# A graph-attention kernel's first stage: order of SyncE's loads and stores, finer query stores, and a block of transposes placed elsewhere on TensorE

## The reference, cut to what matters

```python
h = layernorm(x) @ w_in + b_in             # 3125 x 256
xn = layernorm(h, ln1_g[0], ln1_b[0])
q, k, v = xn @ wq[0] + bq[0], xn @ wk[0] + bk[0], xn @ wv[0] + bv[0]
# then, for each edge: scores from q[dst] and k[src], a softmax over the
# edges of one dst, and the sum of attn * v[src] at dst
```

## Time and profile before

| what | value |
|---|---|
| time, median of 3 runs | 3984.43 us (3982.08 to 3995.94) |
| the profiled execution, time | 4018.18 us |
| its span | 4016.4 us |
| mean granted TensorE clock | 0.733 |
| PE busy in the span | 2360.2 us |
| DVE busy | 2475.5 us |
| ACT busy | 1336.1 us |
| POOL busy | 1837.9 us |
| first gather of the edges | 329.57 us after the span's start |

### The profile page before, as it was taken

The page is one execution under the profiler, slowest core; times in us unless marked ns, Lnnn a source line. Parts: engine busy times, 40 slices in busy tenths (PEclk is TensorE's granted clock), DMA queues, the critical chain, the costliest instruction groups (busy, mean ns, idle before and its releaser), DMA issues. The chain is left out here.

```text
span 4016.4 us, 37654 instructions
## 1 busy us (share of the span) xinstructions
PE 2360.2 (59%) x7337; PEld 1568.5 (39%) x7338; DVE 2475.5 (62%) x3964; ACT 1336.1 (33%) x3899; POOL 1837.9 (46%) x1938
## 2 busy tenths in 40 slices
PE   5863455555555555478773555555555555487697
PEld 3331333333333333256541333333333333366576
DVE  3653777677767777643434777777777777543223
ACT  1111344343434444312112434443434434221132
POOL 4005566666666666221116666666666665111000
PEclk8776676666766667689986666676767667698799
DMA  3226667677666666512126666776666666311100
GB/s 92 64 67 184 180 207 210 197 209 207 207 200 199 203 201 207 149 50 87 60 85 197 199 205 203 208 210 207 206 207 202 203 205 190 90 54 58 43 26 32
DMA packets 293357, 623.34 MB, mean 155 GB/s; under 512 B 51905, under 2 KB 163705, under 8 KB 293184
## 3 DMA queue, kind: packets, MB, share of 16 engines
q0 software_dynamic: 149904, 471.38, 40.4%
q1 hardware_dynamic: 143280, 150.27, 11.8%
HBM read 526.62 MB, written 94.78 MB: 155 GB/s over the span
## 5 line engine op out<-in xcount | busy, mean ns | idle before, releaser
L723 POOL DMA_INDIRECT ring<-kv_table,stage_ix x1760 | 1673.9, 951 | 1020.9 <-issue 601.7
L949 PE MATMUL bank<-qs,hot_q 128*128 x1760 | 710.9, 552 | 616.0 <-issue 304.5
L962 PE MATMUL bank<-ring,hot_w 128*128 128x272 f32 x1760 | 710.2, 543 | 565.8 <-issue 337.2
L1787 DVE TENSOR_TENSOR ring<-ring,bank 128x1024 f32<-128x1024 f32 x440 | 532.6, 1210 | 563.0 <-issue 383.6
L949 PEld LDWEIGHTS bank<-qs,hot_q 128*128 128x128 f32 x1760 | 459.9, 273 | 797.2 <-issue 701.5
L962 PEld LDWEIGHTS bank<-ring,hot_w 128*128 128x128 f32 x1760 | 423.5, 261 | 831.2 <-issue 550.3
L1792 DVE TENSOR_REDUCE s<-ring 128x32 f32<-128x1024 f32 x440 | 532.9, 1211 | 4.2
L1168 ACT ACTIVATE stage_o<-bank 128x272 f32<-128x272 f32 x440 | 167.2, 385 | 530.0 <-remote 300.3
L1153 ACT ACTIVATE s<-bank 128x8 f32<-128x8 f32 x440 | 78.3, 178 | 733.2 <-remote 476.8
L1143 ACT ACTIVATE hot_q<-pos_b,row_of 128x128 f32<-128x128 bf16 x880 | 304.1, 395 | 5.0 <-issue 2.5
L1804 DVE TENSOR_TENSOR bank<-ring,bank 128x512 f32<-128x512 f32 x440 | 301.0, 684 | 0.0
(11 more groups left out here) (293 smaller groups left out, 2377.5 us busy)
## 6 DMA issues: line engine op xcount, KB each, us to landing
agg_d<-stage_o SPq DMA_DIRECT2D x440, 136.0 KB
ring<-kv_table,stage_ix POOLq DMA_INDIRECT x1760
pos_b<-rel_d SPq DMA_DIRECT2D x54, 256.0 KB
kv_table<-ring SPq DMA_DIRECT2D x50, 250.0 KB
h_dram<-ring SPq DMA_DIRECT2D x15, 625.0 KB
ring<-h_dram SPq DMA_DIRECT2D x15, 625.0 KB
q_tab<-ring SPq DMA_DIRECT2D x10, 644.5 KB
ring<-in_x_dram SPq DMA_DIRECT2D x10, 625.0 KB
```

The costliest lines, as they stand in the source:

```text
L723: gps.indirect_dma_start(out=chunk[:, par * G + i, j, :], out_offset=None, in_=table, in_offset=bass.IndirectOffsetOnAxis(ap=stage_ix[:, p ...
L949: mm = ten.matmul(q_bank(third, i)[:, 0:QC], hot_q[:, i % 4, a * P:(a + 1) * P], qs[:, bass.ds(t * QC + a * QC, QC)], start=(a == 0), stop ...
L962: mm = ten.matmul(b_acc[i % 2][:, lo - OWN:MC], hot_w[:, i % 4, :], chunk[:, s, j, lo:ROW], start=(j == 0), stop=(j == QD // 2 - 1), skip_ ...
L1787: tt(k_, k_, q, ALU.mult).then_inc(S["q_used"], 1)
```

## The change

In the first stage SP follows a sequence of its own, `first`. The load of the next `x` comes first, then the store of `h_b`, which waits for the evictions of the projection (`bank_free`) and no longer for `done`. Then come the transfers for the index tables and four tiles of the query table of the batch before. After that each tile's keys and values are stored, and then each tile's queries, as soon as DVE has reduced them. `out_free` is given behind the last query store of the batch, when `h_out` has arrived. ACT no longer waits for `out_free`; it waits for the query and key/value stores of the batch before. The counts of `q_out` change with the number of stores (25 in place of 5 in this stage). On PE, `packs_of_slots` moves from between batches 3 and 4 to the start of the qkv stage of batch 4, behind that batch's turns. Waits of later stages change only in their constants.

```diff
+                def first(it, last):
                     if not last:
-                        if kind == "in":
-                            hold(sp, s["tok"], it * n_tok + BT, S["sp_passed"])
-                            load_x(it + 1)
...
-                    if kind in ("in", "mid"):
-                        for j in range(BT):
-                            hold(sp, s["kvc"], it * BT + j + 1, S["sp_passed"])
-                            sp.dma_start(kv_out.rearrange("(t p) c -> p t c", p=TN)[:, bass.ds(it * BT + j, 1), :],
-                                         kv_b[:, j:j + 1, :]).then_inc(S["kv_out"], 16)
-                    hold(sp, s["done"], it + 1, S["sp_passed"])
...
-                        sp.dma_start(rows(h_dram, it), h_b[:, :, :]).then_inc(S["h_out"], 16)
-                        if kind in ("in", "mid"):
-                            sp.dma_start(rows(q_tab[0:N, :], it), qf).then_inc(S["q_out"], 16)
-                            hold(sp, S["kv_out"], it * (BT * 16) + (no * NBATCH + 1) * BT * 16, S["sp_passed"])
-                        hold(sp, S["h_out"], it * 16 + (no * NBATCH + 1) * 16, s["out_free"])
-                        if kind in ("in", "mid"):
-                            hold(sp, S["q_out"], it * 16 + (no * NBATCH + 1) * 16, S["sp_passed"])
...
+                        hold(sp, s["tok"], it * n_tok + BT, S["sp_passed"])
+                        load_x(it + 1)
+                    hold(sp, s["bank_free"], it * n_used + BT + 3, S["sp_passed"])
+                    sp.dma_start(rows(h_dram, it), h_b[:, :, :]).then_inc(S["h_out"], 16)
+                    if it == 1:
                         sp.wait_ge(S["quads_out"], 16)
...
+                    if it:
+                        hold(sp, S["q_out"], it * (BT * 16), S["sp_passed"])
+                        q_tiles((it - 1) * 4, 4)
+                    for j in range(BT):
+                        hold(sp, s["kvc"], it * BT + j + 1, S["sp_passed"])
+                        sp.dma_start(kv_out.rearrange("(t p) c -> p t c", p=TN)[:, bass.ds(it * BT + j, 1), :],
+                                     kv_b[:, j:j + 1, :]).then_inc(S["kv_out"], 16)
+                        hold(sp, s["dve"], it * D_STEPS["in"] + BT + 2 * (j + 1), S["sp_passed"])
+                        sp.dma_start(q_tab[0:N, :].rearrange("(t p) c -> p t c", p=TN)[:, it * BT + j:it * BT + j + 1, :],
+                                     qf[:, j:j + 1, :]).then_inc(S["q_out"], 16)
+                    hold(sp, S["h_out"], it * 16 + 16, s["out_free"])
...
             pool.wait_ge(S["h_out"], NBATCH * 16)
-            pool.wait_ge(S["q_out"], NBATCH * 16)
+            pool.wait_ge(S["q_out"], NT * 16)
...
                         elif stage == "qkv":
+                            if it == NBATCH - 1:
+                                packs_of_slots()
...
                     rows_of_blocks()
-                elif it == 3:
-                    packs_of_slots()
...
                         elif stage == "qkv":
-                            act.wait_ge(s["out_free"], it + 1)
-                            if kind == "mid" or it:
-                                act.wait_ge(S["q_out"], it * 16 + PASS_NO[kind] * NBATCH * 16)
+                            if it:
+                                act.wait_ge(S["q_out"], it * (BT * 16))
+                                act.wait_ge(S["kv_out"], it * (BT * 16))
```

More of the change, by code:

```diff
@@ L439, in load_v @@
                     sp.dma_start(own_v[:, :, :], rows(kv_in, it, D, ROW)).then_inc(s["x_in"], 16)
-                def batch(it, last):
+                def first(it, last):
                     if not last:
-                        if kind == "in":
-                            hold(sp, s["tok"], it * n_tok + BT, S["sp_passed"])
-                            load_x(it + 1)
[L447 to L454, removed]
-                    if kind in ("in", "mid"):
-                        for j in range(BT):
-                            hold(sp, s["kvc"], it * BT + j + 1, S["sp_passed"])
-                            sp.dma_start(kv_out.rearrange("(t p) c -> p t c", p=TN)[:, bass.ds(it * BT + j, 1), :],
-                                         kv_b[:, j:j + 1, :]).then_inc(S["kv_out"], 16)
-                    hold(sp, s["done"], it + 1, S["sp_passed"])
[L461 to L466, removed]
-                        sp.dma_start(rows(h_dram, it), h_b[:, :, :]).then_inc(S["h_out"], 16)
-                        if kind in ("in", "mid"):
-                            sp.dma_start(rows(q_tab[0:N, :], it), qf).then_inc(S["q_out"], 16)
-                            hold(sp, S["kv_out"], it * (BT * 16) + (no * NBATCH + 1) * BT * 16, S["sp_passed"])
-                        hold(sp, S["h_out"], it * 16 + (no * NBATCH + 1) * 16, s["out_free"])
-                        if kind in ("in", "mid"):
-                            hold(sp, S["q_out"], it * 16 + (no * NBATCH + 1) * 16, S["sp_passed"])
-                        if kind == "mid":
-                            q_tiles(it * 4, 4)
@@ L477, in between @@
-                def between(it):
-                    if it == 0:
+                        hold(sp, s["tok"], it * n_tok + BT, S["sp_passed"])
[3 more added lines that the diff above has]
+                    if it == 1:
                         sp.wait_ge(S["quads_out"], 16)
-                    if it == 2:
+                    if it == 3:
@@ L484, in between @@
                         sp.dma_start(rel_d.rearrange("(a r) e -> r a e", a=2), e_rel).then_inc(S["pens_out"], 16)
-                    if it == 3:
+                    if it == 4:
                         sp.wait_ge(S["pens_out"], 32)
@@ L493, in between, with batch @@
                             positions(x, x, G)
-                    q_tiles(it * 4, 4)
-                sp.sem_inc(s["out_free"], 1)
-                if kind in ("mid", "last"):
-                    load_v(0)
-                if kind != "in":
-                    load_h(0)
[L501 to L509, removed]
+                    if it:
[9 more added lines that the diff above has]
+                    hold(sp, S["h_out"], it * 16 + 16, s["out_free"])
+                def batch(it, last):
+                    hold(sp, s["done"], it + 1, S["sp_passed"])
+                    sp.dma_start(rows(out, it), h_b[:, :, :]).then_inc(S["out_done"], 16)
+                    if not last:
+                        load_h(it + 1)
+                    hold(sp, S["out_done"], it * 16 + 16, s["out_free"])
+                sp.sem_inc(s["out_free"], 1)
+                if kind == "in":
+                    load_x(0)
+                    cuts()
+                    batches(sp, kind, first)
+                    sp.wait_ge(S["pad_out"], 3 * 16)
+                    sp.wait_ge(S["q_out"], NT * 16)
+                    q_tiles((NBATCH - 1) * 4, 4)
+                    q_tiles(NBATCH * 4, QT - NBATCH * 4)
+                else:
+                    load_h(0)
+                    batches(sp, kind, batch)
             def staggered(kind):
@@ L542, in batch @@
                     if kind == "mid":
-                        hold(sp, S["q_out"], it * 16 + (no * NBATCH + 1) * 16, S["sp_passed"])
+                        hold(sp, S["q_out"], it * 16 + (NT + 1) * 16, S["sp_passed"])
                         q_tiles(it * 4, 4)
@@ L758, in _ @@
             pool.wait_ge(S["h_out"], 2 * NBATCH * 16)
-            pool.wait_ge(S["q_out"], 2 * NBATCH * 16)
+            pool.wait_ge(S["q_out"], (NT + NBATCH) * 16)
             table = kv_table2
@@ L1738, in batch @@
                         projected(it + 1, o.proj(it), o.free_proj(it), g, st)
-                    v.wait_ge(S["q_out"], it * 16 + NBATCH * 16)
+                    v.wait_ge(S["q_out"], it * 16 + NT * 16)
                     v.wait_ge(S["kv_out"], it * (BT * 16) + NT * 16)
```

## The result

| kernel | median | runs |
|---|---|---|
| before | 3983.26 us (3976.31 to 4005.15) | 8 |
| changed | 3967.03 us (3958.83 to 3971.75) | 8 |

The ratio of the changed kernel to the one before is 0.9941, with a 95% interval of 0.9923 to 0.9960: 0.6% faster. The forecast was 3955.4 us, or a ratio of 0.9927; its range of 3940 to 3974 holds the measured 3967.03. In two later comparisons the ratio was 0.9937 and 0.9941. The medians of the three comparisons differ by 16.2, 26.6 and 16.2 us; the ratios on record are not the quotients of these medians, and stand for 24 to 25 us. So the change is worth some 16 to 27 us, and the forecast of 29 lies above that but inside the interval of the ratio here, which goes from 16 to 31 us.

The account below looks back on a forecast made before the run. The prediction took the first stage to be bound by SyncE's queue standing behind stores, seen as `out_free`, x and tail stalls. Its terms, -7.0 - 0.3 - 4.4 - 7.4 + 1.2 - 11.1 = -29.0 us, gave 3955.4 us, range 3940 to 3974.

Parts of the forecast that it names:

- the tail: From the last reduce to the first gather: one query tile stands there instead of h and five tiles; -11.1 us.
- the last boundary: Batch 3 to 4: DVE's whole wait of 7.42 us for `out_free` goes; -7.4 us.
- batch 3's own stall: DVE's 5.77 us `out_free` stall in batch 3 goes but becomes a wait for PE; -0.3 us.
- The transposes: Eight transposes moved between batch 4's turns and its qkv matmuls, where PE sets the pace; +1.2 us.
- rival 3: Little arrives: all low bounds together, or a fixed cost per store; sum -9 to -16, 3972 us, chance 0.15.
- the term of -7.0 at batch 1: Batches 0 to 1: the smaller of 8.2 us from earlier evictions and 7.0 us from x; bounds 0 and -8.2.
- the bound of 8.2 us: Batch 0 to 1: DVE goes on 6.8 us earlier and evictions and statistics take 3.66 us instead of 5.12.
- x with a slack of 3.25 us: Batch 1: x lands at 102.2 instead of 105.94, plus DVE's 3.25 us slack against ACT; worth 7.0 us.
- the term of -4.4 at batch 3's x: Batch 3: statistics start 7.2 us earlier, but the first reduce waits for ACT's first tile; -4.4 us.
- rival 1: x stays late in batch 1 behind slow tile stores; sum about -24, 3960.6 us, chance 0.15.
- rival 4: The store queue becomes the bound, binding above 1.5 us extra per tile store; 4015 us, chance 0.05.
- Rival 2: Transposes leave TensorE at 1.2 GHz for the whole qkv of batch 4; sum -17, 3967 us, chance 0.05.

Follow-up runs that it names:

- packs_back: Changed kernel with the eight quad transposes of TensorE back between batches 3 and 4; 3947.72 us, one run.
- one_q_store: Changed kernel with each batch's queries stored by one transfer behind the last reduce instead of tile by tile; 3971.40 us, one run.
- bf16 pair: before_bias3 and bias3_again: the kernel before and the changed kernel, both with the bf16 bias matmul; 3999.66 and 3969.31 us.
- best3: Changed kernel with bf16 bias matmul, quad transposes back between batches 3 and 4, one query store each in batches 0 to 3; 3532.44 us, ratio 0.9861 to before.
- before_bias3: Kernel before with only the qkv bias matmul changed from one-row fp32 to 125-row bf16; 3999.66 us, ratio 0.9972 to before.
- best4: best3 plus filler matmuls, ten ahead of each batch's second turns and four ahead of batch 1's fourth projection; 3957.53 us, ratio 0.9858 to before.
- h_late: Changed kernel with h stored when the batch is done, behind its ten tile stores, as in the kernel before; 3590.55 us, one run.
- bias3: Changed kernel with the qkv bias matmul as bf16, 125 rows deep, instead of one-row fp32; 3539.84 us, ratio 0.9881 to before.
- bias3_again: bias3 repeated, unchanged, on the chip of before_bias3; 3969.31 us, ratio 0.9891 to before.

## Why the prediction was right, and where it was off

**Right: the mechanism, the tail and the last boundary.** `out_free` of batch 3 to 4 gave 7.2 us (term 7.4), the tail 10.4 (term 11.1), batch 3's own stall nothing (term 0.3; the wait for PE stands in its place, as said, and the statistics end at 207.6 in both). The transposes cost 1.3 by the pair of profiles (term 1.2), though packs_back puts it at 3.4. The first gather stands 5.38 us behind the last query store's issue, where 4 to 5 was named. x in batch 1 came at 101.49 (102.2 forecast), though its load was issued 3.1 us later than forecast, so the transfer arithmetic held for back-to-back tile stores too. That speaks against the rule of the Trainium skill (DMA: Bandwidth & Descriptors, the anatomy of one DMA) as I had set it up for rival 3: had each tile store paid a fixed cost of about 2.0 us, x would have come up to 18 us later, on that estimate.

**Off: the term of -7.0 at batch 1.** It measured 0 in the profiled execution, 3.7 in the second and -0.9 (a loss) in the third, by the start of the last reduce; packs_back, whose batch 1 has the same instructions, gained 5.0. The term was the smaller of two bounds, and what failed is the bound of 8.2 us on TensorE's side, in two steps. The first is the price of an issue. DVE went on at 86.40 and not at 83.2, because SyncE's issues took up to 1.50 us each; one_q_store shows it, at 83.33. In the changed kernel DVE still idles 4.49 us for SyncE's queue before these evictions, where the prediction named no such time, and then 5.88 us for x, where it named about 8. From the first eviction to the second turns it took 8.0 us as before, where 1.4 us less was forecast. So the second turns began 3.7 us earlier (94.36 against 98.03) and not 8.2. The second execution, where the clock then did as in the kernel before, gained just these 3.7 us. The second step took TensorE's pace as given and moved it along. In fact TensorE ran at 1.2 GHz for 17 us from 94.36, where before its clock had risen 9.2 us after the turns began, and this took the 3.7 us in the first execution and more than that in the third, where the clock rose at 112.7.

The other bound, x with a slack of 3.25 us, was not the smaller one in any of these executions. In the bf16 pair DVE has no wait for ACT in batch 1, so there is no slack to use; x and the turns both come 4.1 us earlier, and so does the last reduce. With both faults out of the way, fewer issues and the bf16 bias (best3), the last reduce of batch 1 starts at 117.53 against 126.45 in before_bias3: the boundary then gives 8.9 us. The two ran on different chips; best4, on the chip of before_bias3, has 117.40.

**Off: the term of -4.4 at batch 3's x.** It measured 3.2 (and 3.3 in the second execution). ACT's first tile was the releaser, as forecast, but that tile ends when TensorE's matmuls at 1.2 GHz let it, and the clock rose 16.8 us after the turns in place of 9.3. In the third execution it rose after 9.4, and the term is 4.4, as forecast. With the bf16 bias ACT isn't waited for and the same removed wait gives 7.2 (12.65 less 5.41).

**The sum.** 0 - 3.2 - 7.2 + 1.3 - 10.4 is -19.5, the 19.5 between the first gathers. In the bf16 pair the terms are 4.1, 1.3, 7.2, 7.2, -0.4 and 9.0, and the first gathers lie 28.5 us apart, by another route than the forecast 29.0. The agreement of these two sums is in part luck, since 4.1 stands for 7.0 and 7.2 for 4.4. In the third execution of the changed kernel the clock also stayed low for three tiles of batch 2, and its first gather came only 11.6 us ahead of the kernel before; the prediction let batch 2 keep the shift.

**Sums of the prediction that don't come out.** The high bounds of the terms add up to -33.1 and not -35.1 (the low ones to -16.3). The bound of 3.25 us in rival 1 makes its sum about -25 and not -24. In rival 4 the stores, h and x alone are the 31 us of a batch; the query load, 528 KB in the profile, adds about 5 us by the same rate, so the queue would bind from a smaller c. None of this moves the forecast or its range.

**The rivals.** x was not late (rival 1). Rival 2 had the right cause in the wrong place: the clock did stay low, 17 us from the turns in batches 1 and 3 of the first execution, in batch 3 of the second, and 18 and 27 us in batches 1 and 2 of the third. In batch 4 the low stretch is 10.2 us long in the kernel before and in the first two executions; in the third the clock was low before the batch's second turns already and rose 10.5 us after they began. Its 3967 is the measured time, which is a coincidence. Rival 3's size is near, its cause is not. The store queue never became the bound, but h_late shows the edge that it stands on: with h behind the tile stores it costs 18.33 us at one boundary.

**What stays open.** The pairs with and without the bf16 bias show that the clock rises sooner without the one-row fp32 matmuls. Which of their properties matters (one row, fp32, the fewer weight loads that go with them, or the length of the first tile) was not separated, and neither was why one kernel's clock rises at such different times. Single profiles of the changed kernel place the first gather anywhere from 305.67 to 318.01, and the kernel before has only one profile, so the 19.5 of one pair of profiles is itself uncertain by several us; the three comparisons of times are the firmer number. How much of the gain of the bf16 bias comes from the clock and how much from the shorter tile was not measured either.

## What to carry to other kernels

A store or a load taken off the path is worth what the next engine in line can make of it: before the stall's length is written down as a gain, read that engine's granted clock behind the stall, and ask what it would run at if it started earlier. When long runs of TensorE stand at 0.50 while it is busy, look at what it is busy with; here one bias matmul in another form took 21.8 us off the changed kernel (3991.12 to 3969.31; 20 us by the ratios), about as much as the change itself, and only 7.6 us (11 by the ratio) off the kernel before. Store early what is ready early, and large, ahead of many small stores, and cut into tiles only the last store that something waits for.

## What the runs showed of the hardware

- TensorE kept at work can stay at 1.2 GHz: 17 us from 94.36 in the changed kernel's batch 1, with PE busy 2.00 of 2.00 us in the windows from 98 on. Counted from the start of a batch's second turns, the clock rose after 8 to 27 us in the kernel before and the three profiles of the changed one. With bf16 bias matmuls 125 rows deep in place of the one-row fp32 ones it rose after 3.6 to 6.9 us (before_bias3, bias3, bias3_again, best3), in the first qkv tile, in all five batches; in best4 too, no later tile is at 1.2 GHz. The Trainium skill (TensorE: Matmul & The Clock Gate, What's actually happening) has sustained activity release the clock. The trace of bias3_again agrees; in that of the changed kernel the clock stayed at 0.50 for 17 us although PE was busy nearly all the time.
- The time at which the clock rises differs between executions of one kernel: in the changed kernel in batch 1 at 103.4, 111.3 and 112.7, in batch 2 at 164.9, 169.3 and 187.8.
- SyncE's issues of tile stores took 0.26 to 0.30 us with time between them, and 0.58 to 1.50 us from the fourth on in a row (changed kernel, 80.05 to 85.12); the x load, the h store and the query load behind them took 1.59, 4.31 and 5.56 us.
- One chip ran its kernels some 10% faster than the other two (before 3581.90 us against 3988.93 and 4007.29), with ratios as on these (bias3 0.9881 there, 0.9891 on the third).
